# An audio tower on one core: W_o split early, the first group's attention split, loads and softmax steps in another order

## The reference

```
h = patches @ W.T + b
q, k, v = layernorm(h) @ Wq.T, @ Wk.T, @ Wv.T       # 16 heads of 32, rotary embedding on q and k
scores = q k.T / sqrt(32), causal
heavy = the one key with the largest sum of softmax(scores) over the queries
scores = where(heavy key or |i - j| <= 1, scores, lowest)
h = h + (softmax(scores) @ v) @ Wo.T
gate, up = layernorm(h) @ w_gate_up.T               # 2 x 2048
h = h + (silu(gate) * up) @ w_down.T
```

## Time and profile before

| | |
|---|---|
| median of 3 runs | 268.63 us (267.50 to 268.77) |
| profiled execution | 268.19 us, span 266.4 us |
| TensorE matmul busy | 257.1 us (96%) |
| VectorE busy | 169.9 us (64%) |
| ScalarE busy | 108.2 us (41%) |
| GpSimd busy | 48.9 us (18%) |
| mean DMA rate | 145 GB/s |

### The profile page before, as it was taken

One profiled execution on the slowest core, in us unless ns is written; L12 is line 12 of the kernel. 1 busy time (PEld: TensorE's weight loads), 2 busy tenths in 40 slices (PEclk: granted clock), 3 DMA queues, 4 the chain that ended last, 5 costly groups with the idle time before them and its releaser, 6 DMA issues.

```text
span 266.4 us, 5045 instructions
## 1 busy us (share of the span) xinstructions
PE 257.1 (96%) x1909; PEld 213.5 (80%) x1909; DVE 169.9 (64%) x333; ACT 108.2 (41%) x181; POOL 48.9 (18%) x53
## 2 busy tenths in 40 slices
PE   7999999799999999989999999999999999999993
PEld 5466498575887887867888879999999999999992
DVE  1696998997899987899976775633333333343323
ACT  2311212863285454749531053533443333344320
POOL 0116032004001121100100101422222222222210
PEclk9999999999999999999999999999999999999999
DMA  6996003005359999983890050694333344400004
GB/s 220 416 418 220 1 4 122 2 2 100 59 161 232 290 252 288 271 270 135 219 285 12 0 198 5 168 336 127 119 118 118 118 121 126 128 19 0 0 0 118
DMA packets 13154, 38.61 MB, mean 145 GB/s; under 512 B 1864, under 2 KB 1936, under 8 KB 12496
## 3 DMA queue, kind: packets, MB, share of 16 engines
q1 hardware_dynamic: 11120, 32.17, 35.2%
q0 software_dynamic: 1728, 5.81, 11.5%
q10 hardware_dynamic: 288, 0.39, 0.4%
HBM read 31.24 MB, written 1.31 MB: 122 GB/s over the span
## 4 chain that ended last, share of the span: by engine, by line
PE 78%; DMA 8%; DVE 6%; ACT 3%; issue 3%; SPq 1%; POOL 0%; DVEq 0%; POOLq 0%
PE ps L225 49%; PE ps L1345 5%; PE ps L1223 5%; PE ps L1118 4%; DMA wgu<-stage 3%; PE ps L1326 3%; DMA stage<-w_ffn 3%; PE ps L1238 3%; PE ps L1185 3%; PE ps L1144 2%; DMA dims<-w_dims 2%; PE ps L1127 1%; PE ps L1069 1%; PE ps L1155 1%; DVE xT L724 1%
## 5 line engine op out<-in xcount | busy, mean ns | idle before, releaser
L225 PE MATMUL ps<-xT,wgu 128*128 128x384 f32 x384 | 70.5, 339 | 0.2 <-DVE gu L931 0.2
L225 PEld LDWEIGHTS ps<-xT,wgu 128*128 128x128 f32 x384 | 68.1, 188 | 1.8 <-issue 0.6
L931 DVE TENSOR_TENSOR gu<-silu,ps 128x256 f32<-128x256 f32 (+1 forms) x32 | 15.5, 485 | 47.5 <-PE ps L225 44.4
L363 POOL TENSOR_TENSOR wd<-stage,wd 128x512 fp32r<-128x512 f32 x16 | 26.2, 1636 | 77.1 <-ACT wd L431 77.1
L225 PE MATMUL ps<-wd,hT 128*128 128x512 f32 x156 | 38.8, 393 | 0.0
L591 ACT ACTIVATE silu<-ps 128x256 f32<-128x256 f32 (+1 forms) x32 | 14.0, 437 | 52.7 <-PE ps L225 52.2
L225 PEld LDWEIGHTS ps<-wd,hT 128*128 128x128 f32 x156 | 29.0, 188 | 5.4
L225 PE MATMUL ps<-xs,wgu 128*128 128x256 f32 x240 | 31.9, 289 | 0.9 <-DMA wgu<-stage 0.9
L225 PEld LDWEIGHTS ps<-xs,wgu 128*128 128x128 f32 x240 | 28.8, 188 | 4.6 <-issue 4.1
L431 ACT ACTIVATE wgu<-stage 128x1024 fp32r<-128x1024 f32 x20 | 21.1, 1056 | 24.4 <-PE ps L225 23.1
L1345 PE MATMUL ps<-stage,gu 128*128 128x512 f32 x56 | 26.3, 593 | 0.0
(11 more groups left out here) (126 smaller groups left out, 318.3 us busy)
## 6 DMA issues: line engine op xcount, KB each, us to landing
stage<-w_ffn SPq DMA_DIRECT2D x32, 512.0 KB, 4.5
stage<-w_ffn SPq DMA_DIRECT2D x32, 256.0 KB, 4.0
wgu<-stage POOLq DMA_DIRECT2D x6, 512.0 KB, 8.3
wd<-stage POOLq DMA_DIRECT2D x3, 512.0 KB, 7.0
stage<-w_k SPq DMA_DIRECT2D x1, 1024.0 KB, 6.6
stage<-w_q SPq DMA_DIRECT2D x1, 1024.0 KB, 10.1
stage<-w_v SPq DMA_DIRECT2D x1, 1024.0 KB, 12.1
wo<-w_o SPq DMA_DIRECT2D x1, 1024.0 KB, 15.2
```

The lines of the kernel that those rows point to most:

```text
L225: ins = pe.matmul(dst, lhs[a], rhs[b], start=first and n == 0, stop=last and n == 2)
L363: pool.tensor_tensor(dst, src, f32(hi), ALU.subtract).then_inc(done, 1)
L931: dve.tensor_tensor(gu[:, ring, cols], silu[:, ring, cols], ps[:, up, at:at + P * TILES[p]], ALU.mult)\
```

## The change

W_o is loaded into the fourth slot of `stage`, and its own tile is gone. ScalarE splits it right after `folded_bias(1)`, both passes together; GpSimd issues the adding DMA after `spread_bias(0)`. `wo_parts` is kept for all five tiles. `hi_attn(0)` and `hi_attn(1)` write xT and `low_attn(0)` and `low_attn(1)` are new on VectorE; `project_out` runs its three products in the order high x high, high x low, low x high over all of k, and asks for the low attention only before the third. The FFN load of slot 3 waits for the split of W_o, and SyncE's order of the following loads is another. On VectorE only the mask of `SOFTMAX[3]` stays in its place; the rest of its input comes after the first four value products, and the statistics and scales around it change places. On TensorE `project_biases("v", 1)` and `spread_scale(1)` change places. Several tiles lie at other addresses.

```diff
 # memory
-        wo = sb("wo", [P, KT, D])
+        wo_parts = sb("wo_parts", [P, 2, KT, D], F32R)
...
 # SyncE
-            sp.dma_start(wo[:, :, :].rearrange("p k n -> p (k n)"), w_o).then_inc(dma_wo, 16)
+            sp.dma_start(stage[:, 3, :], w_o).then_inc(dma_wo, 16)
...
-            gate_up_load(3)
-            down_load(3)
-            for x in range(3):
+            for x in range(2):
                 sp.wait_ge(fold_bias_mm, x + 1)
                 gate_up_load(x)
                 down_load(x)
-
+            sp.wait_ge(fold_bias_mm, 3)
+            gate_up_load(2)
+            down_load(2)
+            sp.wait_ge(wo_high, 1)
+            sp.wait_ge(dma_wo_low, 16)
+            gate_up_load(3)
+            down_load(3)
+
+            next_gate_up(2)
+            next_gate_up(3)
             next_gate_up(0)
-            for i in range(1, NB):
+            next_gate_up(1)
+            next_down(0)
+            for i in range(4, S2 + 1):
+                next_gate_up(i)
+                next_down(i - 3)
+            next_gate_up(S2 + 1)
+            next_down(S2 - 2)
+            next_down(S2 - 1)
+            next_down(S2)
+            for i in range(S2 + 2, NB):
                 next_gate_up(i)
                 next_down(i - 1)
...
 # GpSimd
             spread_bias(0)
+            low_wo()
             key_add(2)
...
                 low_weights(i)
-            low_wo()
...
 # ScalarE
-                act.activation(wo_parts[:, 1], wo[:, :, :], ACT.Copy, scale=-1.0)
-
-            def hi_wo():
-                act.activation(wo_parts[:, 0], wo[:, :, :], ACT.Copy).then_inc(wo_minus, 1)
+                act.activation(wo_parts[:, 1], whole_wo, ACT.Copy, scale=-1.0).then_inc(wo_minus, 1)
+                act.activation(wo_parts[:, 0], whole_wo, ACT.Copy).then_inc(wo_high, 1)
...
             folded_bias(1)
+            minus_wo()
             folded(2)
...
+            hi_attn(0)
             minus_weights(2)
-            hi_attn(0)
             hi_attn(1)
...
 # VectorE
             softmax_in(2)
-            softmax_in(3)
+            mask(SOFTMAX[3][2])
             softmax_out(2)
             values(0, 7, 6, 5, 4)
+            softmax_in(3, unmasked=False)
+            statistics(3)
             softmax_out(3)
+            low_attn(0)
             values(0, 3, 2, 1, 0)
-            statistics(3)
             statistics(4)
+            statistics(LN2[1])
+            low_attn(1)
+            normalise(LN2[1])
             token_scale(3)
+            statistics(LN2[0])
             token_scale(4)
-            statistics(LN2[1])
-            normalise(LN2[1])
-            statistics(LN2[0])
             normalise(LN2[0])
             tables(1)
...
 # TensorE, project_out
+                for a, b in ((0, 0), (0, 1), (1, 0)):
+                    if a:
+                        pe.wait_ge(attn_lo, units)
+                    for k in range(KT):
+                        ins = pe.matmul(ps[:, WO_BANK[t], :], xT[:, a, k, P * t:P * (t + 1)], wo_parts[:, b, k],
+                                        start=a + b + k == 0, stop=a == 1 and k == KT - 1)
...
             transposes(LN2[1], ("wo", 1))
-            read_out("projection", ("q", 1, 1))
-            pe.wait_ge(apart_set, NT)
-            spread_scale(1)
+            project_biases("v", 1)
...
             transposes(LN2[0], ("wo", 0))
-            project_biases("v", 1)
+            read_out("projection", ("q", 1, 1))
+            pe.wait_ge(apart_set, NT)
+            spread_scale(1)
```

More of the change, by code:

```diff
@@ L132, in audio_tower @@
         whole_mem.close()
-        attn, xf = whole[:, 0], whole[:, 1, :, 0:2 * P]
+        xf = whole[:, 1, :, 0:2 * P]
         xT = sb("xT", [P, 2, KT, TOK], F32R)
@@ L164, in audio_tower @@
         wd = sb("wd", [P, 2, 2, D], F32R)
-        hT = sb("hT", [P, 2, 2, 3 * P], F32R)
-        ob = sb("ob", [P, 3, D])
+        xs = sb("xs", [P, 2, KT, 2 * P], F32R)
         silu = sb("silu", [P, 2, 3 * P])
@@ L169, in audio_tower @@
         scale = sb("scale", [P, NG, NPOS])
-        tcos, tsin = (sb(n, [P, NG, NPOS, HD]) for n in ("tcos", "tsin"))
-        by_cos, by_sin = (sb(n, [P, 2, 4 * DH]) for n in ("by_cos", "by_sin"))
-        v_all = sb("v_all", [P, NG, NPOS, DH])
+        turning_mem = ExitStack()
+        tcos, tsin = (sb(n, [P, NG, NPOS, HD], F32, turning_mem) for n in ("tcos", "tsin"))
+        by_cos, by_sin = (sb(n, [P, 2, 4 * DH], F32, turning_mem) for n in ("by_cos", "by_sin"))
+        turning_mem.close()
+        ob = sb("ob", [P, 3, D])
+        hT = sb("hT", [P, 2, 2, 3 * P], F32R)
+        spare = sb("spare", [P, 2 * DH])
+        k_all, q_all, v_all = (sb(n, [P, NG, NPOS, DH]) for n in ("k_all", "q_all", "v_all"))
         prod = sb("prod", [P, NPOS * (NPOS + 1) // 2, DH])
@@ L179, in audio_tower @@
         hvm = sb("hvm", [P, 2, HQ])
[L180 to L184, removed]
         dma_pat, dma_tok, dma_dims, dma_bias, dma_const = (sem(n) for n in ("dma_pat", "dma_tok", "dma_dims", "dma_bias", "dma_const"))
@@ L206, in audio_tower @@
         probs, pv_dve, pv_mm = sem("probs"), sem("pv_dve"), sem("pv_mm")
+        wo_high = sem("wo_high")
         attn_sb, attn_lo, wo_minus, wo_mm, dma_wo_low = (sem(n) for n in ("attn_sb", "attn_lo", "wo_minus", "wo_mm", "dma_wo_low"))
@@ L392, in low_wo @@
                 pool.wait_ge(wo_minus, 1)
-                pool.dma_start(wo_parts[:, 1], wo[:, :, :], accum_op=ALU.add).then_inc(dma_wo_low, 16)
+                pool.dma_start(wo_parts[:, 1].rearrange("p k n -> p (k n)"), stage[:, 3, :], accum_op=ALU.add).then_inc(dma_wo_low, 16)
             def lo_down(i, ring, slot):
@@ L493, in hi_attn @@
                 a, b = UNITS[u][2]
-                split_hi(xT[:, 0, :, columns(u)] if u >= WHOLE else attn[:, :, columns(u)],
+                split_hi(xT[:, 0, :, columns(u)],
                          ps[:, UNIT_BANK[u], :].rearrange("p (k n) -> p k n", k=KT)[:, :, GB * a:GB * b], attn_sb)
@@ L499, in minus_wo @@
                 act.wait_ge(dma_wo, 16)
-                act.wait_ge(score_sum, NPOS)
-                act.activation(wo_parts[:, 1], wo[:, :, :], ACT.Copy, scale=-1.0)
-            def hi_wo():
-                act.activation(wo_parts[:, 0], wo[:, :, :], ACT.Copy).then_inc(wo_minus, 1)
+                whole_wo = stage[:, 3, :].rearrange("p (k n) -> p k n", k=KT)
+                act.activation(wo_parts[:, 1], whole_wo, ACT.Copy, scale=-1.0).then_inc(wo_minus, 1)
+                act.activation(wo_parts[:, 0], whole_wo, ACT.Copy).then_inc(wo_high, 1)
             def whole_tokens(t):
@@ L638, in _ @@
             hi_weights(13)
-            minus_wo()
             first_pass(11)
-            hi_wo()
             first_pass(12)
@@ L800, in rows, with softmax_in @@
                 return x[:, slice(*part)].rearrange("p i h j -> p (i h) j")
-            def softmax_in(n):
+            def softmax_in(n, unmasked=True):
                 g, masked, part = SOFTMAX[n]
                 if masked:
-                    mask(part)
+                    if unmasked:
+                        mask(part)
                 elif not g:
@@ L848, in mask, with low_attn @@
                 step(dve.tensor_tensor(rows(sm, part), rows(sm, part), rows(keep, part), ALU.min))
+            def low_attn(u):
+                a, b = UNITS[u][2]
+                dve.wait_ge(attn_sb, u + 1)
+                dve.tensor_tensor(xT[:, 1, :, columns(u)], ps[:, UNIT_BANK[u], :].rearrange("p (k n) -> p k n", k=KT)[:, :, GB * a:GB * b],
+                                  f32(xT[:, 0, :, columns(u)]), ALU.subtract).then_inc(attn_lo, 1)
             def values(g, *queries):
@@ L932, in up_product @@
                    .then_inc(gu_prod[p], 1)
[L934 to L939, removed]
             def low_whole():
@@ L1100, in read_out @@
                     pe.wait_ge(attn_sb, n + 1)
-                    if n >= WHOLE:
-                        pe.wait_ge(attn_lo, n + 1 - WHOLE)
+                    pe.wait_ge(attn_lo, n + 1)
                 if stage == "wo":
@@ L1226, in project_out @@
             def project_out(t, units, last):
-                pe.wait_ge(dma_wo, 16)
                 pe.wait_ge(attn_sb, units)
+                pe.wait_ge(wo_high, 1)
+                pe.wait_ge(dma_wo_low, 16)
                 read_out(*last)
[L1230 to L1239, removed]
+                for a, b in ((0, 0), (0, 1), (1, 0)):
[4 more added lines that the diff above has]
+                                        start=a + b + k == 0, stop=a == 1 and k == KT - 1)
                 ins.then_inc(wo_mm, 1)
```

## The result

The changed kernel takes 275.27 us (median of 6 runs, 274.2 to 276.2) against 268.70 for the kernel before: slower, ratio 1.0245 with a 95% interval of 1.0203 to 1.0287. The profiled execution took 275.32 us, its span is 273.5 against 266.4. The direction was forecast, the size was not: 6.6 us more where 3.5 were forecast.

The account below looks back on a forecast made before the run. TensorE, busy 257.1 of 266.4 us, was taken to bound the kernel. The terms +4.15 (value sums delayed), -1.3 (W_o products), +1.5 (tables), -0.9 (loads) gave +3.5, so 272.1 us against the median; range 270.1 to 275.2.

Parts of the forecast that it names:

- The hold: ScalarE's later exponential delays the k and q drains, so TensorE's first value sums start at 57.3, not 53.16: +4.15 us.
- the first rival: TensorE's clock falls in the idle stretch before the value sums, slowing work after it: 273.8, up to 275.6 us; chance 0.34.
- W_o in three products: TensorE's first two output tiles as 12 fp32r matmuls instead of 8 fp32 instructions: 1.3 us less in all.
- The split of W_o moved forward: ScalarE's two early passes and GpSimd's adding DMA fit into idle time before the fold copy and key_add(2): cost nothing.
- One sign: What the profile after should show in the early part: the fold chain before 50 us unmoved.
- The tables: VectorE's tables wait for the later scale matmuls, so the gate product delays down_whole(0): +1.5 us, bounds nothing to 2.0.
- The loads: In the first FFN pass, reordered loads remove TensorE's 0.88 us wait for step 10's DMA sum: -0.9 us, bounds 0 to -0.9.
- second rival: Before the value sums, ScalarE's delay doesn't reach TensorE, as the bank's drain isn't awaited last: 267.1 us; chance 0.07.
- third rival: The value sums are delayed, but later slack makes the tables free and the DMA stall goes: 270.6 us; chance 0.08.
- fourth rival: W_o or its sum is late in the early part, adding 1 to 3 us: 273.1 to 275.1 us; chance 0.05.
- The likeliest case: The forecast for the whole kernel, +3.5 us to 272.1, own range 271.0 to 273.0; chance 0.46.

Follow-up runs that it names:

- experiment 1: Changed kernel with VectorE's softmax order of before restored, the second part's whole input ahead of the first part's normalising: 269.32 us, ratio 1.0019 to the kernel before.
- experiment 2: Kernel before with only the new VectorE softmax order, the second part's input behind the first four value products: 273.93 us, ratio 1.022.
- experiment 3: Changed kernel with added 128-column matmuls on TensorE in front of the first value sums: 277.79 us with 40, 273.16 us with 19.
- experiment 6: Changed kernel with group 1's scale matmuls back before the first gate/up piece, v biases behind it, token scales ahead of the statistics: 274.20 us, ratio 1.0174.
- experiment 4: Changed kernel with 192 bytes of padding in front of xs, no instruction changed: 273.85 us, ratio 1.019 to the kernel before.
- experiment 7: Changed kernel with ScalarE's exponential of the second softmax part moved behind the six drains: 269.83 us, ratio 1.0041 to the kernel before.
- the combined one of 8: Changed kernel with the old softmax order, 192 bytes of padding before xs, and group 1's scale matmuls between tile 1's gate/up pieces: 267.47 us, ratio 0.9953.
- experiment 8: The combined kernel (old softmax order, xs padding, scale matmuls moved; 267.47 us) also run with the first pass's old order of loads: 267.96 us, ratio 0.9965.
- experiment 5: Kernel before with only padding in front of xs: 832 bytes 269.40 us, ratio 1.0023; 320 and 864 bytes, one run each, 268.48 and 268.06 us.

## Why the prediction was wrong, point by point

The sum gave +3.5 us and +6.6 were measured. The step that failed is in the sum: two terms stood in it at nothing, the clock behind the hold (+1.6 us measured) and the new addresses (+1.5 us in the trace). The direction and the four terms that it did have were sound, but for the DMA term, -0.9 where -0.65 was measured.

**The hold: right, place and size.** +4.15 us was forecast and 4.53 less the late start of 0.4 was measured. Only the idle stretch is shorter, 4.72 us instead of 5.6, because TensorE's last projection ended at 52.97 and not at 51.73. Experiments 1 and 2 undo and redo it.

**The clock: named as a rival, left out of the sum.** It stood as the first rival with 0.34, at 273.8 to 275.6 us. The step of the sum that failed here: the gap was taken to cost its length alone, and the slow work behind it was left at nothing. The row of the first matmuls was the evidence, 217 ns for 128 columns where the added matmuls of experiment 3 take 115 to 119, and the forecast gave too much to a granted clock that reads 1.00 in all rows of the kernel before. It cost 1.6 us (4.80 against 3.21), near the 1.7 of the rival, and 19 added matmuls in the idle stretch take it away. That the measured 275.27 lies inside the rival's own 273.8 to 275.6 is luck: the rival didn't have the addresses, and its upper end stood for transposes that wouldn't bring the clock up, while here it came back to 1.00 under them. The Trainium skill (TensorE: Matmul & The Clock Gate, Part 1: The HAM clock gate) says that an idle TensorE falls to 1.2 GHz; this trace agrees, 0.50 from about 54.6 to 61.5 us.

**W_o in three products: right.** 63.50 to 66.38 is 2.88 us against 3.51, and 68.31 to 71.19 the same: twice -0.63, 1.3 together, as forecast.

**The split of W_o moved forward: right, as far as the rows show.** The sum is issued at 25.1 and lands 8.1 later; GpSimd then waits 8.68 us for `key_add(2)`. One sign was missed: the early part should not have moved, and its `fold_bias` matmuls start at 46.48 instead of 46.10. In five profiled executions with the early loads of before they start between 45.74 and 46.67, in nine with the new ones between 46.00 and 47.12. So up to 0.4 us may belong to the change or to chance; that is open. GpSimd's timeline:

```profile
25.07 0.93 POOL L409 DMA_DIRECT2D wo_parts<-stage  x1 [0.31 <-ACT wo_parts L517]
34.69 0.74 POOL L392 TENSOR_TENSOR k_all<-by_cos,by_sin 128x256 f32<-128x256 f32 x1 [8.68 <-DVE by_sin L765]
```

**The tables: right, 1.5 forecast, 1.55 measured** as wait; from the start of the second piece to `down_whole(0)` it is 1.7 more than before. It stays at 1.55 without the hold (experiment 1) and goes when the scale matmuls and token scales stand in front (experiment 6): it is their place.

**The loads: half right.** Forecast -0.9; the wait went from 1.12 to 0.47 us from down part to down part, so -0.65. In seven other kernels with the new order (experiments 1, 4, 6 and 7, the two of 3, and the combined one of 8) it isn't there at all. The reasoning held (the wait comes back with the old order, experiment 8), but in experiment 5 it vanishes with the old order too, so that it can't simply be added to other terms.

**The addresses: missed altogether.** The diff moves xs from 199776 to 135072 and the forecast put no price on that. The 240 + 96 matmuls that read xs last 7 ns longer each by their medians; they overlap, and in the trace that makes 12 steps by 0.13 = 1.5 us. Experiment 4 takes 1.56 us of it back in the trace and 1.4 in the time. Experiment 4, without it, has 273.85, where the clock rival stood at 273.8: this is the term that puts the time past the range's upper end of 275.2, by 0.07 us.

The second, third and fourth rivals are out: the value sums do wait for the drain, the tables weren't free and the hold wasn't given back, W_o came in time. The likeliest case's own range, 271.0 to 273.0, didn't follow from the bounds that were named: tables from 0 to 2.0 and the DMA stall from 0 to -0.9 give 270.6 to 273.5. The measured time lies outside either.

## What to carry to other kernels

When a step is moved on one engine, read every other engine's list for the step that waits for it, and for what stands behind that step: the price is what was queued behind, not the step. A gap of 4.7 us on TensorE cost its length and then the slow matmuls after it, where gaps of 1.4 us at the same place did not (the kernel before); cheap matmuls that filled it, and ended before it did, took back the second part. And a diff that only moves tiles has to be priced too: look at the offset of the moving against the stationary operands modulo 512 bytes.

## What the hardware showed that was not expected

Matmuls of 256 fp32r columns, each with a fresh 128x128 weight load, ran at 114 ns from load to load, and at 120 ns when the moving tile lay at the same byte offset modulo 512 as the weights, in both kernels and with no instruction changed; 32 bytes off it was 117 ns. The layouts without the loss (the kernel before, and the changed one with 192 bytes of padding) both have 192 bytes between the two offsets modulo 512. No other distance was tried, and why the place matters no run shows.

The clock did not fall at a fixed time after the last matmul. In the changed kernel its mean of 0.77 between 53 and 56 us means half speed from about 54.6, 1.6 us after the last matmul. By the same working it fell 1.8 us after it in experiment 2, 3.2 in experiment 6 (0.68 between 56 and 57 us) and 3.7 in experiment 4 (0.59 between 57 and 58 us). The first value sums, under nearly the same hold, took 4.80, 4.42, 5.33 and 4.38 us. So the price of the fall differs from execution to execution: 1.4 to 2.4 us over the 2.98 of full clock. In the kernel with 40 added matmuls it was low even before the hold, where TensorE had only paused for 1.46 us among small matmuls; the kernel before idles for 1.43 us in front of its value sums and keeps 1.00. Stretches of the kernel with 40 added matmuls:

```profile
50.00:51.00 1.00, 0.33 (x9) 0.33 (x13) 0.93 (x3) 0.00 (x0) 0.00 (x0) 0.96 0.00 0
51.00:54.00 3.00, 3.00 (x51) 2.36 (x43) 2.90 (x4) 0.00 (x0) 0.00 (x0) 0.50 0.02 5
```

That pause, near 49 us, is in six of the nine profiled executions with the changed kernel's early loads, 0.4 to 1.5 us long, and the profile puts it down to "issue"; none of the five with the early loads of before has it. The hold covered it here. Its cause stays open.
